# Two-layer adaLN transformer on one core: first layer's q and k in two 32-bit parts instead of three bf16 parts, head halves as 64-row pairs, a shared ring of PSUM banks

## The reference

```
h      = layernorm(x) * (1 + ca) + sa                  # ca, sa: per batch, from c @ wmod
latent = h @ Wc_down                                   # 128 -> 64
q      = (latent @ Wq_up).reshape(B, T, 16, 8)         # 16 heads of width 8
k, v   = split(latent @ Wkv_up)                        # one k and one v of width 8 for all heads
att    = softmax(where(causal, q . k / sqrt(8), -inf))
x      = x + ga * ((att @ v) @ Wc_proj)
```

## Time and profile before

| | us |
|---|---|
| median of 3 runs | 949.28 |
| the runs | 943.24, 1445.51, 949.28 |
| span of the profiled execution | 963.0 |
| of it, first stage (attention of layer 0) | 0 to about 458 |
| experts, then second layer | about 458 to 963 |

### The profile page before, as it was taken

How to read it: one execution, slowest core, us unless ns; L and a number is a source line. 1 busy time by engine, 2 the same in 40 slices (tenths; PEclk the granted TensorE clock), 3 DMA queues, 4 the chain that set the end, 5 groups by cost and what they waited for, 6 DMA issues and landing times.

```text
span 963.0 us, 16301 instructions
## 1 busy us (share of the span) xinstructions
PE 803.9 (83%) x5862; PEld 388.1 (40%) x5862; DVE 585.6 (61%) x1505; ACT 448.1 (47%) x726; POOL 407.0 (42%) x533
## 2 busy tenths in 40 slices
PE   4687999889898989896688699779975778999887
PEld 3223333334333334333334244334433445665555
DVE  3676767666767676726676233330238758887885
ACT  1002555444545454573322243333324758887763
POOL 7221012323232322031002477878755469886523
PEclk9657999899999899998799799888995889999999
DMA  5211344144434232131300123333330011111111
GB/s 129 68 37 41 83 133 99 35 99 144 95 63 98 58 87 69 29 94 43 102 0 12 35 37 44 46 42 46 33 46 22 5 26 26 25 33 24 25 28 33
DMA packets 69110, 52.88 MB, mean 55 GB/s; under 512 B 20640, under 2 KB 62056, under 8 KB 68456
## 3 DMA queue, kind: packets, MB, share of 16 engines
q1 hardware_dynamic: 59176, 44.28, 18.1%
q0 software_dynamic: 9856, 7.58, 6.0%
HBM read 31.76 MB, written 18.23 MB: 52 GB/s over the span
## 4 chain that ended last, share of the span: by engine, by line
PE 51%; DVE 20%; issue 9%; POOL 7%; DMA 6%; ACT 3%; SPq 2%; another core or an unknown queue 1%; POOLq 1%; DVEq 0%; ACTq 0%
PE bank L404 8%; PE bank L387 7%; DVE MX L793 6%; PE ps_s L362 5%; POOL d_acc L1290 5%; PE ps_o L1494 3%; PE b1ps L1984 3%; PE b1ps L1995 3%; PE bank L407 2%; DVE R L1386 2%; PE ps_s L371 2%; PE ps_h L1482 2%; DMA Q<-d_q 2%; PE b1ps L2008 2%; DVE hit L1324 1%
## 5 line engine op out<-in xcount | busy, mean ns | idle before, releaser
L793 DVE TENSOR_REDUCE MX<-bank 128x1 f32<-128x512 f32 (+3 forms) x352 | 216.3, 639 | 85.5 <-PE bank L407 81.3
L578 ACT ACTIVATE PR<-ps_s 128x1024 f32<-128x1024 f32 x160 | 158.9, 1022 | 156.0 <-PE ps_s L371 89.9
L404 PE MATMUL bank<-K,Q 96*128 96x512 bf16 (+3 forms) x512 | 136.4, 327 | 31.6 <-DVE MX L793 16.5
L404 PEld LDWEIGHTS bank<-K,Q 96*128 96x128 bf16 x512 | 44.5, 102 | 153.8 <-DVE MX L793 113.2
L362 PE MATMUL ps_s<-Q,K 99*128 99x512 bf16 x320 | 97.6, 394 | 1.8 <-DMA Q<-d_m 1.8
L1290 POOL DMA_INDIRECT d_acc<-Y,idx x56 | 87.6, 1564 | 20.4 <-issue 16.5
L407 PE MATMUL bank<-maskT,identb 128*128 128x128 bf16 (+2 forms) x352 | 92.7, 263 | 0.0
L1280 POOL DMA_INDIRECT XG<-d_tab,idx x56 | 53.7, 959 | 90.2 <-DVE idx L1395 73.2
L387 PE MATMUL bank<-PR,VE 128*32 128x512 f32 x640 | 90.2, 638 | 0.0
L1494 PE MATMUL ps_o<-H,w 128*128 128x512 f32 x176 | 87.8, 649 | 0.0
L1614 ACT ACTIVATE H<-ps_h,b1T 128x512 f32<-128x512 f32 x88 | 60.1, 687 | 46.1 <-PE ps_h L1482 39.2
(11 more groups left out here) (346 smaller groups left out, 1397.7 us busy)
## 6 DMA issues: line engine op xcount, KB each, us to landing
Q<-d_q SPq DMA_DIRECT2D x24, 384.0 KB
d_q<-qs SPq DMA_DIRECT2D x24, 128.0 KB, 2.3
X<-L_attn_x SPq DMA_DIRECT2D x8, 256.0 KB, 4.8
w<-L_ffn_W SPq DMA_DIRECT2D x8, 256.0 KB, 4.4
d_acc<-zrow SPq DMA_DIRECT2D x1, 2048.0 KB, 9.3
w<-L_ffn_W SPq DMA_DIRECT2D x1, 2048.0 KB, 9.1
AC<-d_acc SPq DMA_DIRECT2D x8, 256.0 KB, 2.8
d_y<-ysb SPq DMA_DIRECT2D x112, 18.0 KB
```

The costliest lines, as they stand in the source:

```text
L404: nc.tensor.matmul(ps_mx[G % 2][:, x * w:(x + 1) * w], Q[b % QB][0:KR, h, P * g:P * g + P], K[b % QB][0:KR, 0:w], start=(x == 0), stop=Fal ...
L578: nc.scalar.activation(PR[t % 2][:, 2 * half:2 * half + 2, :], ps_s[half][:, :].rearrange("p (a f) -> p a f", a=2), ACT.Exp, scale=DH ** - ...
L793: nc.vector.tensor_reduce(MX[b % 2][:, c:c + len(hs)], ps_mx[G % 2][:, 0:len(hs) * w].rearrange("p (x w) -> p x w", w=w), AX_X, ALU.max).t ...
```

## The change

Parts are now two, in `float32r`, a 32-bit type in which a producer rounds what it writes. `NPR` = 2 x 2 x 8 = 32 rows of products; with 2 rows for the maximum `KM` = 36. Since that fits in 64 rows, `K` is held twice, at partitions 0 and 64, and `Q` holds heads 0 to 7 at partition 0 and heads 8 to 15 at partition 64. Every K-Q matmul becomes one of a pair at tile positions (0, 0) and (64, 0), each of the pair into a bank of its own. The mask of the maxima is added in two turns with 64-row tiles (`identb` x `maskT`, `identX` x `maskX`) instead of one matmul of 128 rows.

```diff
-PARTS = 3
+PARTS = 2
 NPR = PARTS * PARTS * DH
-KR = 96
+KR = NPR + PARTS
...
-    ps_s = [a0.enter_context(nc.psum_tensor(f"ps_s{i}", [P, 1024], F32)) for i in range(2)]
-    ps_mx, ps_y, ps_misc = bank[0:2], bank[2], bank[3]
+    ring = [a0.enter_context(nc.psum_tensor(f"ring{i}", [P, 512], F32)) for i in range(NRING)]
+    ps_s = [a0.enter_context(nc.psum_tensor(f"ps_s{i}", [P, 512], F32)) for i in range(NSB)]
...
+            U = 4 * (NSTEP * b + s) + 2 * pair
+            for r in range(2):
+                o = 64 * r
+                if U + r >= NSB:
+                    pe.wait_ge(S["exp_done"], U + r - NSB + 1)
+                last = nc.tensor.matmul(ps_s[(U + r) % NSB][:, :], K[b % QB][o:o + KM, P * i:P * i + P],
+                                        Q[b % QB][o:o + KM, 4 * pair:4 * pair + 4, P * g:P * g + P],
+                                        start=True, stop=(i < g), tile_position=(o, 0), skip_group_check=(i == g))
...
+                for x in range(len(heads[0])):
+                    for r in range(2):
+                        if x == 0:
+                            acquire(("max", G + r))
+                        nc.tensor.matmul(out_[r][:, x * w:(x + 1) * w],
+                                         Q[b % QB][64 * r:64 * r + KR, heads[r][x] % HR, P * g:P * g + P],
+                                         K[b % QB][64 * r:64 * r + KR, 0:w], start=(x == 0), stop=False,
+                                         tile_position=(64 * r, 0), skip_group_check=True)
...
-                    if x < 2 and 0 <= n < NB:
-                        scores_T(n, s, x)
-                    if x >= 2 and 0 <= t < NSTEP * NB:
-                        values(t, x - 2)
+                    if x in (0, 2) and 0 <= n < NB:
+                        scores_T(n, s, x // 2)
+                    if x == 1 and 0 <= t < NSTEP * NB:
+                        values(t)
...
-                    for half in range(2):
+                    for x in range(4):
...
-                nc.vector.tensor_tensor(qr[:, :], m[:, :], qs[:, 0, :], ALU.subtract).then_inc(S["misc_free"], 1)
-                free((kind, b))
-                nc.vector.tensor_copy(qs[:, 1, :], qr[:, :]).then_inc(S["q2_rdy"], 1)
+                nc.vector.tensor_tensor(qs[:, 1, :], m[:, :], qs[:, 0, :].bitcast(F32), ALU.subtract).then_inc(free, 1)
...
-                    pool.wait_ge(S["q2_rdy"], b + 1)
-                    nc.gpsimd.tensor_tensor(qs[:, 2, :], qr[:, :], qs[:, 1, :], ALU.subtract).then_inc(S["q3_rdy"], 1)
...
-                    for c in range(PARTS):
-                        sp.dma_start(Q[b % QB][24 * c:24 * c + 24].rearrange("r h q -> r (h q)"),
-                                     bass.AP(d_q[par].tensor, 0, [[NH * T, PARTS * DH], [1, NH * T]])
-                                     ).then_inc(DS[f"q_in{par}"], 16)
+                    for r in range(2):
+                        for c in range(PARTS):
+                            o = 64 * r + PARTS * DH * c
+                            sp.dma_start(Q[b % QB][o:o + PARTS * DH].rearrange("r h q -> r (h q)").bitcast(F32),
+                                         bass.AP(d_q[par].tensor, r * HR * T, [[NH * T, PARTS * DH], [1, HR * T]])
+                                         ).then_inc(DS[f"q_in{par}"], 16)
```

423 lines of the change are left out of this document (236 added, 187 removed).

## The result

The changed kernel takes **970.8 us** (median of 4 runs, 964.2 to 973.9) against 953.4 us for the kernel before in the same session: ratio 1.021, 95% interval 1.015 to 1.027. It is slower, by about two per cent; whether by more or by less than two isn't settled. 870 us was forecast.

A forecast was written before the change was run, and what follows sets the result against it. TensorE bounds steps 0 to 7 now, VectorE close behind; VectorE would bound them after. Gains of 57 (six batches), 7.8 (batch 6), 4.5 (batch 7) and 9.5 (start) make 79 us: 949.3 - 79 = 870 us, range 850 to 892.

The forecast's parts named there:

- Does a pair really run together, and in one pass?: Scores and maxima: 32-bit pairs assumed side by side in one pass, at bf16's 0.22 us for 512 columns.
- Rival 1: Scores and maxima: queued 32-bit weight loads bound the pairs, 0.14 to 0.28 us more each; 890 us, chance 0.17.
- Steps 0 to 7, 29 us: Each batch's steps 0 to 7: VectorE's 27 us plus 2 us for imperfect fit, 29 instead of 36.85 us.
- TensorE's 25.2 us of work: Steps 0 to 7: TensorE's 33.3 us less 3.5 scores, 3.9 maxima, 1.2 masks, plus 0.5 for switches.
- VectorE's "27 us": Steps 0 to 7: VectorE's 29.64 us less 0.6 for casts and about 2 for back-to-back reductions; becomes the bound.
- Rival 4: TensorE, waiting more often, stays at half clock in every stretch: a batch 54 us, total 990 us, chance 0.03.
- The tail, 9.7 us: Each batch's tail: TensorE's own work 10.7 falls to 9.2 us, taken as 9.7 for low clock; 11.55 before.
- Q's load has 9 fewer microseconds in which to hide but starts 1.7 us sooner: Q's load in each batch: less time to hide, but an earlier start after q's subtraction; no time added.
- the rows still land 8.3 us after the last reduction: Tail, m through DRAM: 0.5 us saved on VectorE, 0.63 us added by a fourth load, so landing unchanged.
- rival 5: A late transfer, Q's load or m's rows, sets the batch at 43 to 44 us: 905 us, chance 0.04.
- Batch 7, -4.5 us: Last batch: halved scores give 4.4 us, masks 1.6, ScalarE's activations rise to 26 to 27; 4.5 us gained.
- The start, -9.5 us: Before batch 0's first scores: four banks, shorter waits and smaller Q load bring them to 73.5 instead of 83.1 us.

The follow-up runs named there:

- e1: Changed kernel, with TensorE reading K and Q of scores and maxima as bf16 (upper halves of the same bytes): 936.3 us, 0.985 of the kernel before.
- e6: Changed kernel with layer-norm statistics moved to step 9 and q's store and Q's loads on GpSimd's queue: 947.3 us, 0.988 of the kernel before.
- e8: e6 plus twelve thrown-away 512-column matmuls in the tail before TensorE's wait for m's rows: 959.2 us, 0.996 of the kernel before.
- e10: Changed kernel with three bf16 parts and six products, statistics at step 9, q's store and Q's loads on GpSimd's queue: 886.6 us, 0.936 of the kernel before.
- e2: Changed kernel with q's store and Q's loads on GpSimd's queue, with semaphores of their own: 965.4 us, 1.011 of the kernel before.
- e3: Changed kernel with half of Q's load, leaving out half of the products of parts: 947.0 us, 0.993 of the kernel before.
- B: Suspect: 32-bit operands with longer weight loads; tried alone by reading K and Q as bf16 in the changed kernel: 936.3 us, 0.985 of the kernel before.
- C: Suspect: the granted clock; tried alone by moving the statistics to step 9 in the changed kernel: 953.0 us, 0.989 of the kernel before.
- A: Suspect: Q's load is late; tried alone by moving q's store and Q's loads to GpSimd's queue in the changed kernel: 965.4 us, 1.011.

## Why the prediction was wrong

The stage was to become 79 us shorter and became 18 us longer. Of these 97 us the tails are some 40 (+29.4 against -11), steps 0 to 7 some 36 (-18.7 against -55), batch 7 some 14 and the start some 7. Three steps failed: the tail's sum, which let Q's load hide and m's rows land as before; the 0.22 us for a pair of 32-bit matmuls; and the clock, which the sum supposed to stay at 1.00.

- **"Does a pair really run together, and in one pass?"** Yes to both, and the 0.22 us that was taken for it was still too low: 0.34. The Trainium skill, FP8 and Floating Point Precision, TensorE Precision Notes, sets a 4-byte value read and truncated against the four passes of true FP32; one record and 0.34 us for 512 columns, against two records and 0.91 us for f32, agree with that. Rival 1 (weight loads bound the pairs) comes nearest to what happened. Its 0.12 us for an f32 load is the distance between starts; each of those eight loads is recorded with 186 to 193 ns, like this type's 187, and they overlap. Nor do the two tiles' loads queue, as it supposed: they run at the same time. The rule of the Trainium skill that it quoted (TensorE: Matmul & The Clock Gate, Weight-path perf modes: fast weight load is for 128 weights of a type that is not FP32) agrees with 187 against 98 ns. e1 prices the type at 34 us, where the rival had 20.
- **Steps 0 to 7, 29 us.** Where the clock stayed up they took 33.1 (after) and 30.9 (e6, e8), with bf16 pairs 29.2 to 29.4 (e10). TensorE's 25.2 us of work was 28.4 to 29.4 with 32-bit loads and 26.5 with bf16; VectorE's "27 us" was 27.4. The two microseconds between 33 and 31 are the statistics: "in step 0 VectorE has reductions and two sets of statistics" was seen, and taken as 2 us of friction. What was missed is that a ring which is full behind them stops TensorE for 1.5 us, and that the clock then falls in two batches of four.
- **Rival 4, the clock falls (chance 0.03).** It was judged by a stretch at the program's start and by batch 7, which before ran at 1.00. Batch 7 now has 0.56 for its first 20 us. Two of the six stretches of steps 0 to 7 ran at 0.83, all tails at 0.56 to 0.67. The rival's price of 990 supposed it in every stretch. Its reason against, batch 7 at 1.00, was read from 412 us on, where batch 6 was still at work; the clock of batch 7 itself was 1.00 too.
- **The tail, 9.7 us.** The largest error: 13.9 to 17.8 us in the first six tails. Two sentences fail. "Q's load has 9 fewer microseconds in which to hide but starts 1.7 us sooner": the shrinking cover was named and never priced, although the start shows that such a load takes 9.6 us from issue to use. From its issue right at the end of step 7, it can't be there in a tail of 9.7 us. And it did not start sooner: `d_q` was issued 0.3 us after GpSimd's subtraction before, but K's loads ended just then too (300.46, `d_q` 300.50), and they stand ahead of q in SyncE's queue; in the changed kernel `d_q` goes out 4.4 us after q's subtraction, as soon as K's loads are issued. Second, "the rows still land 8.3 us after the last reduction" left out what is under way when m is stored: now Q's load, 8.5 us for m's store instead of 3, and 5.4 to 7.0 us even with the load on another queue (e2). This is rival 5 (chance 0.04). Removing part of it alone brings little, as e2 shows. The third part of the tail is the clock: 0.56 to 0.67 in all seven, where the sum went by 0.85.
- **Batch 7, -4.5 us.** It became 9.2 us longer, and even e10, at a clock of 0.95, has 42.4 us against 41.3. ScalarE is the engine to look at. Its row of before (414.72 to 440) and that of e10 (348.16 to 375):

```profile
L578 ACT ACTIVATE PR<-ps_s 128x1024 f32<-128x1024 f32 x19 | 18.5, 1023 | 4.8 <-PE ps_s L371 2.5 <-PE ps_s L362 2.3
```

```profile
L660 ACT ACTIVATE PR<-ps_s 128x512 f32<-128x512 f32 x37 | 20.0, 601 | 6.4 <-PE ps_s L441 3.2 <-PE ps_s L430 3.1
```

  With the copies (2.4 us in both) it is busy 20.9 of 25.3 us before and 22.4 of 26.8 in e10: TensorE's saved time found an engine that had 1.5 us more to do, and in e10 TensorE waits 1.4 us for a bank of the three and 2.2 us for the copies. This was read from rows, not tried.
- **The start, -9.5 us.** Only 2 us came. The transposition of batch 0's maxima moved from 74.6 to 70.8 us, but the first wait for Q is 5.1 us there (3.9 before). In e10, which starts at 78.4, it is 7.8 us, and with half the load (e3) the scores start at 74.4: the start belongs to this load.
- **What was right.** The parts of the sum about work: one pass, tiles side by side, VectorE's 27 us, ScalarE hidden in steps 0 to 7. With the three effects largely gone (32-bit operands, clock, Q's place in the queue) e10 has batches of 38.5 to 39.3 us. It supports the sum's form, but its work is other than the forecast's, and its tails still wait for Q, so part of this closeness is chance. Added one at a time the effects are unequal, by the ratios in per cent of the kernel before: alone 3.6 (B), 3.2 (C), 1.0 (A); A on top of C 0.1, on top of B 0.9, on top of both 2.2. By the medians the same are 34, 18 and 5 us alone and 22 us for the last; each ratio is sure to about 0.5 to 0.8.

Left open: why the clock falls after one wait of 1.5 us and not after an equal one, and why it stays low for longer with 32-bit operands; whether their cost is in the loads or in the streaming; and whether m's store ahead of Q's load would help, which was not tried.

## What to carry to other kernels

When a change shortens a stretch that covers a transfer, price the transfer by its measured time from issue to use against the new stretch, and list what else is transferred meanwhile: a small store issued during a large load pays too, on another queue as well. A narrower type can be worth more than fewer products: three bf16 parts with six products fit the same 64 rows as two 32-bit parts with four, and their pairs follow one another sooner (0.22 against 0.34 us). And repair everything that idles TensorE in the dense stretch before judging one repair, since the granted clock can take back what a single one gives.
